# A fused transformer block in fp32: two TensorE products of every third attention step change places

## The reference

```python
x = x + 0.5 * ffn(layernorm(x), ...)      # x: 1 x 4096 x 256
x = x + attention(layernorm(x), ...)
x = x + 0.5 * ffn(layernorm(x), ...)

# attention, 16 heads of 16 features
Q, K, V = (einsum('bsd,hkd->bhsk', x, W) for W in (WQ, WK, WV))
scores = einsum('bhqd,bhkd->bhqk', Q, K) / sqrt(16)
scores = where(causal, scores, -inf)
out = einsum('bhsv,hdv->bsd', softmax(scores) @ V, WO)
```

## Time and profile before

| | before |
|---|---|
| median of three runs | 1912.75 us |
| profiled execution, its own time | 1913.25 us |
| its span in the trace | 1911.5 us |
| TensorE matmuls (PE) busy | 1869.8 us, 98% |
| TensorE weight loads (PEld) busy | 1310.3 us, 69% |
| VectorE (DVE) busy | 1634.6 us, 86% |
| ScalarE (ACT) busy | 1416.7 us, 74% |
| GpSimd (POOL) busy | 562.6 us, 29% |
| granted TensorE clock, mean | 0.995 |

### The profile page before, as it was taken

One profiled execution on the slowest core, in us unless ns is written; L12 is line 12 of the kernel. 1 busy time (PEld: TensorE's weight loads), 2 busy tenths in 40 slices (PEclk: granted clock), 3 DMA queues, 4 the chain that ended last, 5 costly groups with the idle time before them and its releaser, 6 DMA issues.

```text
span 1911.5 us, 62638 instructions
## 1 busy us (share of the span) xinstructions
PE 1869.8 (98%) x24312; PEld 1310.3 (69%) x24312; DVE 1634.6 (86%) x3631; ACT 1416.7 (74%) x2884; POOL 562.6 (29%) x1056
## 2 busy tenths in 40 slices
PE   4999999899999999999999999999999999999999
PEld 3788888666666666666666666666666666679998
DVE  7756666799999999999999999999999999747662
ACT  5312221589898998989999998999999899875433
POOL 4100100032232333223233322323332232235444
PEclk9999999899999999999999999999999999999999
DMA  7111221212112111211121121111112121101110
GB/s 204 52 54 53 76 82 54 79 42 54 40 51 45 48 46 41 56 40 51 47 47 45 41 55 41 52 47 46 46 41 55 42 52 34 56 26 67 67 45 23
DMA packets 82840, 102.43 MB, mean 54 GB/s; under 512 B 16752, under 2 KB 45168, under 8 KB 82544
## 3 DMA queue, kind: packets, MB, share of 16 engines
q1 hardware_dynamic: 81920, 98.03, 18.3%
q10 hardware_dynamic: 624, 0.40, 0.1%
HBM read 68.46 MB, written 29.36 MB: 51 GB/s over the span
## 4 chain that ended last, share of the span: by engine, by line
PE 94%; DVE 3%; ACT 1%; DMA 1%; POOL 0%; issue 0%; SPq 0%; POOLq 0%; ACTq 0%; DVEq 0%
PE PS L1385 31%; PE PS L1369 30%; PE PS L1254 9%; PE PS L1204 8%; PE PS L1234 7%; PE PS L1433 5%; PE PS L1310 1%; PE PS L1170 1%; PE PS L1228 1%; DVE OA L1008 1%; DMA PG<-w_exp_t 1%; ACT OA L698 0%; POOL QT L667 0%; DVE OA L912 0%; ACT OA L742 0%
## 5 line engine op out<-in xcount | busy, mean ns | idle before, releaser
L788 ACT ACTIVATE PG<-PS 128x512 f32<-128x512 f32 (+3 forms) x2304 | 1135.0, 568 | 113.3 <-PE PS L1369 84.6
L1032 DVE TENSOR_REDUCE MXP<-PS 128x1 f32<-128x512 f32 x1686 | 1041.5, 681 | 23.7 <-PE PS L1254 16.8
L1254 PE MATMUL PS<-KT,QT 48*128 48x512 f32 (+5 forms) x2304 | 782.6, 430 | 2.7 <-DVE MXP L1032 2.2
L1369 PE MATMUL PS<-QT,KT 50*128 50x512 f32 (+3 forms) x2304 | 732.2, 423 | 2.1 <-DMA QT<-MT 1.5
L1385 PE MATMUL PS<-PG,VH 128*17 128x128 f32 x16896 | 652.8, 275 | 0.5 <-POOL PG L623 0.2
L1385 PEld LDWEIGHTS PS<-PG,VH 128*17 128x17 f32 x16896 | 432.8, 97 | 201.9 <-issue 178.2
L1369 PEld LDWEIGHTS PS<-QT,KT 50*128 50x128 f32 x2304 | 359.1, 184 | 271.8 <-ACT PG L788 198.6
L1254 PEld LDWEIGHTS PS<-KT,QT 48*128 48x128 f32 (+1 forms) x2304 | 373.9, 185 | 22.4 <-DVE MXP L1032 8.9
L1028 DVE CUSTOM_DVE_ANT_0 PS<-PS,MASK 128x128 f32<-128x128 f32 (+3 forms) x512 | 242.0, 511 | 38.6 <-PE PS L1254 35.8
L623 POOL TENSOR_SCALAR_AFFINE_SELECT PG<-PG 128x128 f32<-128x128 f32 x512 | 144.2, 292 | 407.4 <-ACT PG L788 396.8
L716 ACT ACTIVATE PG<-PS,GB 128x512 f32<-128x512 f32 x128 | 90.2, 706 | 154.6 <-PE PS L1204 154.6
(11 more groups left out here) (118 smaller groups left out, 1536.6 us busy)
## 6 DMA issues: line engine op xcount, KB each, us to landing
QT<-q_parts SPq DMA_DIRECT2D x256, 64.0 KB
KT<-k_parts SPq DMA_DIRECT2D x256, 64.0 KB
q_parts<-OA SPq DMA_DIRECT2D x16, 512.0 KB, 2.8
k_parts<-OA SPq DMA_DIRECT2D x16, 512.0 KB, 3.7
QT<-q_parts SPq DMA_DIRECT2D x256, 32.0 KB
KT<-k_parts SPq DMA_DIRECT2D x256, 32.0 KB
o_parts<-OS SPq DMA_DIRECT2D x128, 64.0 KB
OA<-o_parts SPq DMA_DIRECT2D x32, 256.0 KB
```

The lines of the kernel that those rows point to most:

```text
L788: nc.scalar.activation(PB[u % P_BUFFERS][:, q0:TILE], bank(s_bank(u))[:, q0:TILE], ACT.Exp, scale=1.0 / DH ** 0.5).then_inc(exp_done, 1)
L1032: nc.vector.tensor_reduce(dst, bank(b), AX.X, ALU.max).then_inc(mx_red, 1)
L1254: mm(bank(b, w), q[0:rows, (BT * place(j) + qs) * P:(BT * place(j) + qs + 1) * P].bitcast(f32r), k[0:rows, c * TILE:c * TILE + w].bitcast( ...
L1369: mm(bank(s_bank(u))[:, q0:TILE], kt[0:SM, kb * P:(kb + 1) * P].bitcast(f32r), qt[0:SM, place(j) * TILE + q0:(place(j) + 1) * TILE].bitcas ...
```

## The change

In the third step of each group, the maximum product is issued ahead of the score product. The first two steps keep their order. Nothing is added or removed, and no wait is altered. Only TensorE's order changes; the orders of VectorE, ScalarE and the DMA queue are the same.

```diff
             for g in range(GROUP_N):
                 for u in group_units(g):
-                    scores(u)
-                    ahead_maximum(u)
+                    if u % GROUP < GROUP - 1:
+                        scores(u)
+                        ahead_maximum(u)
+                    else:
+                        ahead_maximum(u)
+                        scores(u)
                 if g == 1:
                     pe.wait_ge(att_init, 2)
                 for u in VALUES_IN[g]:
```

## The result

The changed kernel takes 1923.09 us, the median of five runs (1922.09 to 1924.66), against 1912.75 us (1912.68 to 1913.71). The ratio, estimated from all runs, is 1.0048, with an interval of 1.0036 to 1.0059, which is 7 to 11 us; the two medians are 10.3 us apart. +3.4 us was forecast, and the range ended at 1921.

The account below looks back on a forecast made before the run. VectorE was seen near its limit, TensorE's groups at least 1.68 us plus holds of the third pair. 16 x 0.02 + 15 x 0.27 = 4.4 us, less 1.0, gave +3.4 us, 1916.1; range 1911 to 1921.

Parts of the forecast that it names:

- Both products wide: Third steps with both products 512 columns wide: cost 0, whether VectorE or ScalarE holds them.
- Narrow maximum products: VectorE-held third steps, maximum product narrower than score product: losses 0.16, 0.11, 0.11, 0.05 in groups 6, 17, 25, 44.
- Now a 512-wide score product is left, which takes 0.42: Group 6: value products 0.42 behind the maximum product's load instead of 0.26, a loss of 0.16 us.
- It absorbs all but about 0.02 of the 0.16: VectorE's 0.14 us idle before group 10's first item swallows group 6's delay, leaving 0.02 us in each of 16 heads.
- The gain of group 0: ScalarE-held third step with a 256-wide score product: value products 0.07 us earlier, 15 x 0.07 = 1.0 us gained.
- rival 1: ScalarE-held groups: score load cannot pass a waiting matmul, each group 0.03 to 0.07 us longer; 1924, chance 0.14.
- rival 2: Third step: second maximum load waits for the first's stream in the same rows; 30 us slower, 1943, chance 0.03.
- rival 3: Maximum product freed from ScalarE's wait cuts VectorE's idle time: -8 us, 1905, chance 0.11.

Follow-up runs that it names:

- narrow_back: The changed kernel with the old order back in the eight third steps whose maximum product is narrower than the score product; 1914.96 us beside 1914.16 for the kernel before.
- only_g6_loads_first: The kernel before with the new order in group 6 alone and the score product's wait for keys moved ahead of the maximum product; 1916.3 us.
- score_narrow_only: The kernel before with the new order only in third steps whose score product is narrower than the maximum product; 1914.47 us beside 1914.37.
- loads_early_after: The changed kernel with all waits for keys and queries of a group's three steps moved to the group's start; 1917.78 us, ratio 1.0014.
- only_g6: The kernel before with the new order only in the third step of group 6 of each head; 1918.07 us beside 1914.37.
- loads_early: Waits for keys and queries moved to each group's start, in the kernel before (1913.34 us beside 1914.17) and in the changed kernel (1917.78 us).

## Why the prediction was wrong

- **Both products wide: right.** Where VectorE holds, both loads start together and the value products follow 0.43 behind. Where ScalarE holds, nothing changed in the group's length. narrow_back, with the change in 40 of 48 groups, cost 0.10 us a head.
- **Narrow maximum products: right in kind and place.** Groups 17, 25 and 44 cost 0.116, 0.117 and 0.056 when changed alone; 0.11, 0.11 and 0.05 were forecast, and all of it carries to the end of the head as the prediction said.
- **Group 6 was mis-sized: 0.16 forecast, 0.27 measured.** The step "Now a 512-wide score product is left, which takes 0.42" left out that its load starts 0.13 behind the maximum load. The cause is the wait for keys that the score product carries there (only_g6_loads_first: 0.1 back). The order rows show it, `[waits exp_done,ld_ck0]`, and I gave it no price. Groups 2 and 14 have such a wait too, and with 0.06 each they make what narrow_back's head has over that of score_narrow_only, 0.11 us; with the waits at the start of the group (loads_early_after) it is gone. Group 28's +0.10 is no loss of its own but the gain of group 27 taken back.
- **The step that failed most is "It absorbs all but about 0.02 of the 0.16".** Group 6, late by 0.28 in only_g6, leaves 0.23 us a head. I let VectorE be late and TensorE's group 10 be on time. But group 7 passes its delay on through its exponentials to the third score product of group 8, so TensorE reaches group 10 late as well, and only 0.07 of VectorE's idle time there is free to give.
- **The gain of group 0 was counted and does not stay.** score_narrow_only has it in group 0 (-0.07), and group 2 takes it back (+0.07). I had seen this for groups 15, 24 and 27, and group 0 obeys the same rule.
- **The rivals.** The late load behind a matmul that waits for its rows (rival 1) did not occur: in groups held by ScalarE the score load stayed where it was (group 33: +0.53 before and after), and with it the same-row rule of rival 2 is out: the third maximum load came at +0.35 there. In group 33 the maximum product was freed from ScalarE's wait as rival 3 has it, by 0.19 us, and it gave nothing: the groups 29 to 43, most of them held by ScalarE, keep their length within 0.01 us each.

Per head and over 15 heads, the forecast of +3.4 us is corrected by about +3.1 for group 6 (0.23 for 0.02), +1.0 for group 0, and +1.5 for the other groups (narrow_back's 0.10). That makes 9.0 us where the attention stage shows 8.4: the parts are not quite additive. With the 1.6 us of scatter ahead of the stage it covers the 10.3 us. The two loads_early kernels say the same from the other side: with the waits out of the way the new order costs 0.26 us a head, 3.9 us in 15 heads, near the forecast. What the sum lacked is above all the price of the satisfied waits and what a longer delay of group 6 carries on. Part of that nearness is luck, since the gain of group 0 counted in it is not there. Not settled is group 25, which grew by 0.20 in the full change and by 0.117 alone; 0.08 of it is group 24's gain taken back, and I read that only from score_narrow_only, where group 25 grows by 0.08 with its own order unchanged.

## What to carry to other kernels

When two independent products of an engine that takes them in the program's order change places, ask which of them stands last ahead of the next stage and how long that one takes when nothing of it is hidden; the narrow one should be last. Count each product's waits, the satisfied ones too, and put those that are always satisfied where the engine is not held. Idle time of one engine absorbed a delay here only as far as the other engines of the loop arrived on time; follow the delay through each of them before writing it off.

## What was not expected of the hardware

- A satisfied wait is not free on TensorE. Beside a held one it costs about 0.07 us, because one of the two stands on an instruction of its own, 51 ns long, and the load follows 0.08 behind that: one in every third step made 1.0063 of the kernel before (0.75 us a head) and added 0.81 us a head to the changed one.
- It costs that both where the held wait is that of the product ahead (group 13 with the additional wait: 978.94 to 979.01) and where it is the product's own (groups 37 and 41: 0.06 longer in either kernel).
- Two weight loads for different rows of the array start within 0.01 us of each other when both are free (974.96 and 974.97), in either order, and the time from the later load to the value products is 0.42 to 0.43 us in either order.
- The granted clock falls for 3.4, 6.8 or 10.2 us at the start of the attention stage, behind 1.4 to 1.5 us of waiting, from one kernel to another with the same code there; 3.4 us more or less of it are about 1.3 us of the time.
